# GpSimd's gathers written as a loop, with their index columns brought by transfers of SyncE

## The reference

```
h = relu(layernorm(x));  x = x + L0(h)   # attention, 4 heads: needs xl[src] + xr[dst] per edge
h = relu(layernorm(x));  x = x + L1(h)   # out = segsum(w*sup[src], dst) + segsum(w*sup[dst], src) + bias
h = relu(layernorm(x));  x = x + L2(h)   # two general_conv: segsum(x[src], dst) @ W_msg + x @ W_self
h = relu(layernorm(x));  x = x + L3(h)   # attention, 8 heads: softmax over s_u[src] + s_v[dst]
```

## Time and profile before

| | us |
|---|---|
| median of 3 runs | 10865.6 (10844.58 to 10889.47) |
| profiled execution, its own time | 10864.05 |
| its span | 10862.3 |
| fetch0, from its first to its last gather | 257 to 1656 |
| l1 | 4703 to 5925 |
| l2a | 5984 to 7143 |
| l2b | 7254 to 8410 |
| fetch3 | 8637 to 9892 |

### The profile page before, as it was taken

How to read it: one execution, slowest core, us unless ns; L and a number is a source line. 1 busy time by engine, 2 the same in 40 slices (tenths; PEclk the granted TensorE clock), 3 DMA queues, 4 the chain that set the end, 5 groups by cost and what they waited for, 6 DMA issues and landing times. The chain is left out here.

```text
span 10862.3 us, 133142 instructions
## 1 busy us (share of the span) xinstructions
PE 6182.5 (57%) x24674; PEld 4882.1 (45%) x24675; DVE 5021.5 (46%) x12212; ACT 1331.7 (12%) x3940; POOL 5577.6 (51%) x4923
## 2 busy tenths in 40 slices
PE   4798885774656666644444555555555532222565
PEld 2687874553544444433333344344434432222454
DVE  6444446886544444445554222242222311114888
ACT  2111111221322222200000000010000300000000
POOL 3656550000068888876665677747777156662000
PEclk9778777997877777766766677777776655555798
DMA  4555555553067777754443333323333156663354
GB/s 151 171 163 172 166 159 189 168 170 97 2 115 104 104 104 105 105 128 129 129 130 97 96 89 86 90 80 88 89 89 88 57 169 194 190 194 100 124 169 155
DMA packets 835111, 1359.28 MB, mean 125 GB/s; under 512 B 112278, under 2 KB 488660, under 8 KB 834980
## 3 DMA queue, kind: packets, MB, share of 16 engines
q0 software_dynamic: 315328, 634.04, 26.3%
q1 hardware_dynamic: 385684, 562.46, 16.0%
q10 hardware_dynamic: 133968, 161.50, 4.7%
HBM read 943.05 MB, written 414.50 MB: 125 GB/s over the span
## 5 line engine op out<-in xcount | busy, mean ns | idle before, releaser
L993 POOL DMA_INDIRECT rows_in<-table,gidx x2352 | 2471.9, 1051 | 1241.6 <-issue 646.6
L1090 PE MATMUL ps_p<-rows_in,hot 128*128 x5280 | 1767.9, 494 | 1671.2 <-DVE regionC L956 555.3
L1090 PEld LDWEIGHTS ps_p<-rows_in,hot 128*128 128x128 f32 x5280 | 1245.8, 247 | 2154.4 <-issue 1944.2
L1711 POOL DMA_INDIRECT scatter_sums<-regionC,idx x880 | 1386.5, 1576 | 307.1 <-issue 247.8
L956 DVE TENSOR_TENSOR regionC<-regionC,ps_p 128x257 f32 (+2 forms) x1320 | 558.4, 423 | 1537.1 <-DVEq L953 968.2
L1453 PE MATMUL ps_p<-regionA 128*128 128x265 f32 (+1 forms) x3520 | 965.8, 434 | 429.5 <-DVE regionB L956 197.6
L1002 POOL DMA_INDIRECT regionC<-table,gidx x784 | 807.8, 1030 | 674.7 <-POOLq L1001 440.9
L993 POOL DMA_INDIRECT regionB<-table,gidx x784 | 830.3, 1059 | 570.1 <-POOLq L991 340.4
L1453 PEld LDWEIGHTS ps_p<-regionA 128*128 128x128 f32 x3520 | 732.9, 213 | 662.0 <-DVE regionB L956 242.9
L1914 PE MATMUL psS<-dst_scores,regionA 128*128 x1760 | 393.3, 362 | 884.7 <-PEq L1912 464.2
L1914 PEld LDWEIGHTS psS<-dst_scores,regionA 128*128 128x128 f32 x1760 | 383.5, 330 | 894.5 <-issue 894.5
(11 more groups left out here) (302 smaller groups left out, 7577.9 us busy)
## 6 DMA issues: line engine op xcount, KB each, us to landing
regionA<-edge_rows SPq DMA_DIRECT2D x880, 256.0 KB, 3.3
edge_rows<-regionB SPq DMA_DIRECT2D x196, 512.0 KB
edge_rows<-regionC SPq DMA_DIRECT2D x392, 256.0 KB
regionC<-srcrow_d SPq DMA_DIRECT2D x220, 256.0 KB
scatter_sums<-zero_rows ACTq DMA_DIRECT2D x8, 6400.0 KB, 42.3
regionA<-scatter_sums ACTq DMA_DIRECT2D x49, 1024.0 KB
rows_in<-table,gidx POOLq DMA_INDIRECT x2352
regionB<-rrow_d ACTq DMA_DIRECT2D x110, 256.0 KB
```

The costliest lines, as they stand in the source:

```text
L993: g.indirect_dma_start(out=rows_of(k % (ring * EG)), out_offset=None, in_=table, in_offset=bass.IndirectOffsetOnAxis(ap=gidx[:, k:k + 1], ...
L1090: x = te.matmul(ps[(u.c * VG + j) % NB][:, 0:width], hot[:, b, 2 * j + k, :], at_tile(G, slot[j] * 2 + k), start=k == 0, stop=k == 1)
L1711: g.indirect_dma_start(out=scat, out_offset=bass.IndirectOffsetOnAxis(ap=idx[:, b, j:j + 1], axis=0), in_=sums[:, b, j, :], in_offset=None ...
```

## The change

POOL's gathers now stand in hardware loops. A gather needs its index column at a fixed address, so the columns come through a small buffer `gather_rows` of two halves, each for half a ring of groups: 16 columns in fetch0, 12 in the plain passes, 24 in fetch3. SP fills a half with one transfer from `gidx` (`load_indices`): the first two before its loop (`first_indices`), then one after the last group of a half has landed, for the groups that will go where that half is (`landed_indices`). POOL waits for `idx_full` at the first group of each half (`index_columns`). There are 49 such transfers in fetch0, 66 in each plain pass and 33 in fetch3, 280 in all. POOL still waits itself for the used count, now with one register load for each group. SP's loops leave the last ring's turns written out (`steady`).

```
-        def landed_groups(sp, s_rows, ring, keep=None):
+        def landed_groups(sp, s_rows, ring, idx, keep=None):
             def group(u):
                 ...
                 sp.sem_inc(s_landed.sem, 1)
-            for t_ in turns(sp, NEG, ring, 0):
+                landed_indices(sp, u, ring, EG, idx)
+            first_indices(sp, ring, EG, idx)
+            for t_ in turns(sp, NEG, ring, 0, steady=NEG - ring):
                 group(t_.at(0))
+        def load_indices(sp, u, ring, per, idx):
+            b, half = (u.c // (ring // 2) % 2, ring // 2)
+            n = half * per if not isinstance(u.val, int) else min(half * per, ET - u.val * per)
+            if n > 0:
+                sp.dma_start(idx[:, b, 0:n], gidx[:, bass.ds(u.val * per, n)]).then_inc(idx_full[b], 16)
+        def landed_indices(sp, u, ring, per, idx):
+            if u.c % (ring // 2) == ring // 2 - 1:
+                load_indices(sp, U(u.val + ring // 2 + 1, u.c + ring // 2 + 1), ring, per, idx)
+        def index_columns(g, u, ring, per, idx):
+            b, at = (u.c % ring // (ring // 2), u.c % (ring // 2) * per)
+            if at == 0:
+                g.wait_ge(idx_full[b], 16)
+                g.sem_inc(idx_full[b], -16)
+            return [idx[:, b, at + j:at + j + 1] for j in range(per)]
         def gather(...):
-            regs = registers(g, f'by_visit_{name}', VG)
-            for n in range(NEG):
-                    if old % VG == 0:
-                        done = of_visits(g, visits_by[0:1, :], old, regs, NV)
-                    g.wait_ge(used.sem, done[old % VG] + (used.base + unused))
+            regs = registers(g, f'by_visit_{name}', 1)
+            def fetch(u):
+                    done = of_visits(g, visits_by[0:1, :], u.val - ring, regs, NV)[0]
+                    g.wait_ge(used.sem, done + (used.base + unused))
                     ...
+                rows = index_columns(g, u, ring, EG, idx)
+            for t_ in turns(g, NEG, ring, ring):
         def gather_eights(...):
+            def fetch(u):
+                g.wait_ge(free[b], 1)
+                g.sem_inc(free[b], -1)
+                rows = index_columns(g, u, ring, GS, idx)
+            for t_ in turns(g, ET // GS, ring, 0):
 ... attention_fetch3, SP:
                 def keep(u):
                     ...
+                    landed_indices(sp, u, R3, GS, idx)
+            first_indices(sp, R3, GS, idx)
-            for t_ in turns(sp, NG3, R3, 1):
+            for t_ in turns(sp, NG3, R3, 1, steady=NG3 - R3):
```

More of the change, by code:

```diff
@@ new lines, in landed_indices, with first_indices @@
+        def landed_indices(sp, u, ring, per, idx):
+            if u.c % (ring // 2) == ring // 2 - 1:
+                load_indices(sp, U(u.val + ring // 2 + 1, u.c + ring // 2 + 1), ring, per, idx)
+        def first_indices(sp, ring, per, idx):
+            for n in (0, ring // 2):
+                load_indices(sp, U(n, n), ring, per, idx)
+        def index_columns(g, u, ring, per, idx):
[4 more added lines that the diff above has]
+            return [idx[:, b, at + j:at + j + 1] for j in range(per)]
@@ L987, in gather @@
+        def gather(g, name, table, rows_of, s_rows, ring, used, unused, idx, kept=None):
+            top_row = g.to_reg(NP - 1)
+            regs = registers(g, f'by_visit_{name}', 1)
+            def fetch(u):
+                b = u.c % ring
+                if u.c >= ring:
+                    done = of_visits(g, visits_by[0:1, :], u.val - ring, regs, NV)[0]
+                    g.wait_ge(used.sem, done + (used.base + unused))
                     g.sem_inc(group_free, 1)
                     if kept:
-                        kept(g, old, b)
+                        kept(g, u.val - ring, b)
@@ L990, in gather @@
                     g.wait_ge(group_free, 1)
                     g.sem_inc(group_free, -1)
-                for k in range(n * EG, n * EG + EG):
-                    g.indirect_dma_start(out=rows_of(k % (ring * EG)), out_offset=None, in_=table, in_offset=bass.IndirectOffsetOnAxis(ap=gidx[:, k:k + 1], axis=0), bounds_check=top_row, oob_is_err=True).then_inc(s_rows[b].sem, 16)
-        def gather_eights(g, table, rows_of, s_rows, ring, free):
-            top_row = g.to_reg(NP - 1)
[L997 to L1002, removed]
+                rows = index_columns(g, u, ring, EG, idx)
@@ new lines, in fetch, with gather_eights @@
+                for j in range(EG):
+                    g.indirect_dma_start(out=rows_of(b * EG + j), out_offset=None, in_=table, in_offset=bass.IndirectOffsetOnAxis(ap=rows[j], axis=0), bounds_check=top_row, oob_is_err=True).then_inc(s_rows[b].sem, 16)
+            for t_ in turns(g, NEG, ring, ring):
+                if t_.inside or t_.c < NEG:
+                    fetch(U(t_.val, t_.c))
+        def gather_eights(g, table, rows_of, s_rows, ring, free, idx):
+            top_row = g.to_reg(NP - 1)
+            def fetch(u):
+                b = u.c % ring
+                g.wait_ge(free[b], 1)
+                g.sem_inc(free[b], -1)
+                rows = index_columns(g, u, ring, GS, idx)
+                for j in range(GS):
+                    g.indirect_dma_start(out=rows_of(b * GS + j), out_offset=None, in_=table, in_offset=bass.IndirectOffsetOnAxis(ap=rows[j], axis=0), bounds_check=top_row, oob_is_err=True).then_inc(s_rows[b].sem, 16)
+            for t_ in turns(g, ET // GS, ring, 0):
+                fetch(t_.at(0))
@@ L1008, in plain_pass @@
                 G = sb('rows_in', [P, RG * EG, width], F32, ctx)
+                idx = sb('gather_rows', [P, 2, RG // 2 * EG], I32, ctx)
                 hot = sb('hot', [P, 2, GS, P], F32, ctx)
@@ L1040, in _ @@
                             sp.sem_inc(aux_full[1], 1)
-                        landed_groups(sp, s_rows, RG)
+                        landed_groups(sp, s_rows, RG, idx)
                     @block.scalar
@@ L1073, in _ @@
                     def _(g):
-                        gather(g, name, table, lambda k: G[:, k, 0:D], s_rows, RG, s_add, NB)
+                        gather(g, name, table, lambda k: G[:, k, 0:D], s_rows, RG, s_add, NB, idx)
                     @block.tensor
@@ L1244, in kept @@
                             g.wait_ge(s_keep[b].sem, (n - b) // RG0 * 16 + 16 + s_keep[b].base)
-                        gather(g, 'att0', T0, lambda k: G[:, k, :], s_rows, RG0, s_used, 0, kept)
+                        gather(g, 'att0', T0, lambda k: G[:, k, :], s_rows, RG0, s_used, 0, idx, kept)
                     @block.scalar
@@ L1858, in attention_fetch3 @@
                 psS = [bank(f'psS{b}', ctx) for b in (0, 1)]
+                idx = sb('gather_rows', [P, 2, R3 // 2 * GS], I32, ctx)
                 with phase() as block:
@@ L1888, in _ @@
                     def _(g):
[L1889 removed]
+                        gather_eights(g, T4, lambda k: G[:, k, :], s_rows, R3, free3, idx)
                     @block.scalar
```

6 lines of the change are left out of this document (2 added, 4 removed).

## The result

The changed kernel takes 10949.0 us (median of 5 runs, 10922.0 to 10969.4) against 10865.6; the ratio is 1.0078, 95% interval 1.0061 to 1.0095. It is slower by 83 us, a little more than the 54 us up to which I had called it no change. The time lies in the range, but it moved, and the predicted 10890 us is 59 us short. The profiled execution (10922 us, span 10920.3) is the fastest of the five, so its trace shows 58 us of the 83.

A forecast was written before the change was run, and what follows sets the result against it. PE was taken to set fetch0, POOL nearly to set l2a and l2b, and fetch3 to hang on POOL and DVE together. 10864 + 16 (starts) + 10 (fetch3) = 10890 us; range 10815 to 11020.

The forecast's parts named there:

- the forecast that nothing measurable happens: Whole kernel: 10835 to 10915 us, no change by the 0.5% (54 us) that a measurement can tell; chance 0.55.
- Rival B: fetch3: index transfer behind write-backs, POOL locks to the halves, 13.1 us a group against 12.4; +64 us, 10944; chance 0.25.
- What fetch3 waits for: fetch3: DVE waits 565.2 us for PE's scores, and POOL stops 213 us for places that DVE's reads give free.
- Loops and register loads at 0: All passes: 132 backward branches cost 0 (upper end 330 us); about 587 more register loads, hidden behind queued gathers, cost 0.
- Index transfers hidden in the plain passes and fetch0: Plain passes: a transfer needs 5 us of 15.8, 10 spare; fetch0 has 15 spare; cost 0.
- Starts: First gather of each pass waits for its index: fetch0 9, l1 3, l2a and l2b 2 each, fetch3 0; sum 16 us.
- fetch3 at +10: fetch3: some stops grow from 7.1 to 15.5 us, but longer runs of gathers follow; +10 us, ends -80 and +230.
- the 290 at which I would have called myself wrong: fetch3: sign against the prediction if POOL's stops sum to over 290 us; they were 213 before.
- every second or third stop falls on the first group of a half: fetch3: halves of three groups beat against runs of four, so only such stops wait for the index, about 8 us more.
- The upper end of +230 us: fetch3: all 31 waits grow by 7.5 us and nothing is given back.
- my own sign of too thin a cover: l2a or l2b longer by more than 10 us: register loads or index transfers less well hidden than taken.

The follow-up runs named there:

- first_direct: Changed kernel, but the first ring of groups in each pass is gathered straight from gidx, as before; 9976.7 us, ratio 1.0000 to the kernel before.
- late_two: Changed kernel with each half's index transfer in the three plain passes going out two groups later; 11037.2 us, ratio 1.0055 to the kernel before.
- after_burst: Changed kernel with 24 added writes of zeros on DVE in every third turn of fetch3; 10444.5 us, against 10449.3 for the kernel before with the same writes.
- f3_early: Changed kernel with a four-part index buffer in fetch3, each part asked for one ring earlier; 10001.5 us, ratio 1.0025 to the kernel before.
- before_max: Kernel before with one more register operation (max with 0) behind each loaded count that PE, DVE or POOL waits for; 9977.8 us, ratio 0.9997.

## Why the prediction was right, and where not

- **Sign and size.** Predicted +26 us, measured +83 (1.0078); in the faster condition +35. The range held because it was wide; the forecast that nothing measurable happens, to which 0.55 was given, did not. Rival B's 10944 us is 5 us from the median, but by luck: B had 64 us in fetch3, and the trace shows 22.
- **What fetch3 waits for:** misread from the start. I took the 565.2 us of the earlier trace rows for DVE waiting for PE's scores. PE had them ready: the last section shows that DVE's own sequencer stood still, for 603 us after PE's signals. So the kernel before is held up in fetch3 by something that neither the prediction nor a rival had.
- **Loops and register loads at 0:** right, by first_direct and the issue gaps in the faster condition. The loads are 758 now, 567 more, not 587.
- **Index transfers hidden in the plain passes and fetch0:** right as far as the runs reach. The four waits of over 1 us put down to line 998 inside l2a and l2b of the changed kernel are not the index's: the transfers that they needed had gone out 17.5 to 19.3 us before. late_two took 10.6 us of cover away in the plain passes and lost nothing that shows; in fetch0 the cover was not touched.
- **Starts.** The sum was near, 21 us in the profiled pair where I had 16, but by terms that cancel. The single starts were too large (2.6 us from issue to gather, not 3.9; fetch0 5.8 us late, not 9), and what I let each pass swallow was too much: "of which I count 3" for l1, before which POOL stands 6.8 us longer, and which is as long as before, and "I count 2 each" for l2a and l2b, 5.5 and 2.9. Where POOL sets a pass from its first gather to its last, a late start is lost whole, and I had said myself that l2b is within a tenth of that. In the faster condition the starts with fetch3's first stop are 33 us of 35.
- **fetch3 at +10:** the mechanism of a single stop was right, release, write-backs, index, with 15 to 16 us for a full stop, and so was the argument that stops lock to the ring, as rival B had it. What was mis-sized is the sum, +22 us in place of +10. POOL's stops come to 237 us, short of the 290 at which I would have called myself wrong. The assumption that "every second or third stop falls on the first group of a half" is wrong in kind: 15 of the 15 index waits stand at the first group of the ring, and after_burst shows that such stops by themselves can cost nothing. (The upper end of +230 us also counted 31 waits where the earlier trace rows has 27.)
- **What is still open.** l2a and l2b were longer by 12 and 15 us in the one profile of the slower condition, by 3 and -2 in the faster one. Over 10 us was my own sign of too thin a cover, but neither the index waits above nor late_two bear that out. It is the largest part of what the prediction missed. The median lies another 27 us above the profiled execution. No kernel with the plain passes alone as before ran in the slower condition, so I can't say whether this is the change (its 280 small transfers are some 40,300 packets more, 875,388 against 835,111) or the scatter of that condition, whose runs spread over 47 us for the changed kernel, and over 6 to 24 us for one kernel in the other.

## What to carry to other kernels

When a program is shortened by a loop whose operands come by transfer, look at the first iteration: the steady transfers hide behind the ring, the first does not, and each pass pays it in full if the engine that waits is the one that sets the pass. Written-out first turns can use the old operands and cost nothing (first_direct). And a transfer that refills a buffer should not queue behind bulk write-backs on the same engine; where it must, ask for it a ring earlier (f3_early, whose first stop fell from 22.0 to 13.2 us).

And before an engine is said to wait for another, set the end of its wait against the moment at which the other was done.

## What the runs showed of the hardware

The same kernel has two conditions, 9976 and 10980 us in two sets on one chip. TensorE's granted clock is not what differs in fetch3: it is 0.50 in both, with 383 against 393 us of PE busy for nearly as many matmuls, and yet the pass takes 1256 or 1071 us. In fetch0 it does differ, 0.94 against 0.79; whether that is a cause or follows from longer pauses of PE, no run shows. What differs in fetch3 is how long instructions of the sequencers take. Line 1868 of SP in the kernel before (the write-backs of fetch3; duration min/median/max in ns), slower condition:

```profile
L1868 SPq FUSED_REGOPS  x360: 3/49/1637, 8803.9 to 9900.2; - x180
L1868 SPq MOVE edge_rows<-regionC x360: 3/29/1533, 8804.0 to 9900.3; - x180
```

The same line in before_max, faster condition:

```profile
L1871 SPq FUSED_REGOPS  x360: 46/46/66, 8054.3 to 9004.1; - x180
L1871 SPq MOVE edge_rows<-regionC x360: 29/29/38, 8054.4 to 9004.2; - x180
```

A register move that takes 29 to 38 ns takes up to 1533 ns in the slower condition. The median is 29 ns in both, so it is some of them that are slow. In the earlier trace rows this was the 12.94 us for four write-backs while POOL gathered, against 2.74 while it stood. I had read these 13 us as what a stream of gathers always does to SP; in before_max POOL gathers all the time, and it doesn't.

DVE's sequencer stands longer still. PE's rows around the 22.04 us for which DVE stands until 9112.86 in the earlier trace rows, kernel before:

```profile
9080.67 3.58 PE L1914 MATMUL psS<-dst_scores,regionA 128*128 x16 [3.61 <-issue]
9091.26 3.58 PE L1914 MATMUL psS<-dst_scores,regionA 128*128 x16 [7.02 <-PEq L1910]
9117.37 0.80 PE L1914 MATMUL psS<-dst_scores,regionA 128*128 x3 [22.54 <-PEq L1912]
```

The scores that DVE takes at 9112.86 were finished by 9084.3, and those of the group behind them by 9094.8; it is then PE that waits for DVE. Over the whole of fetch3, with each of the 110 waits at line 1939 set against the PE signal that it asks for, DVE's sequencer stands there for 607 us, and for 603 of them the signal had been given (48 times over 1 us, up to 25). In the changed kernel it is 615 of 619 us, in late_two 626 of 630, in before_max 5 of 8, never over 1 us. The same line as the waits of before_max have it:

```profile
DVE logits L1946 <- DVEq L1942: 40.9, 98, 3.0
```

So in the slower condition it is the sequencers, DVE's above all, and not PE, for which fetch3 waits: DVE's reads come late, the places come free late, and POOL stops for them. What makes the sequencers stand, and what brings the condition about, no run shows.
